# Expert weights and bias rows loaded at other places, the lower split in eight pieces, dest after the lower half, division first at the close

## The reference, cut to what matters

```python
y = (A * p + Bc * vt) / (A * q + Bc)          # per time step; the division of this case
x = layernorm(x + (sigmoid(r) * y) @ Wo.T)    # x1
logits = x @ Wg + bg
score, idx = top_k(logits, 2)                 # softmax over the two
h = tokens @ W1[e] + b1[e]                    # 256 -> 1024
a = gelu(h) if e % 2 == 0 else silu(h)
y_e = a @ W2[e] + b2[e]                       # 1024 -> 256
out = layernorm(x + sum of score * y_e over the two experts)
```

## Time and profile before

| | |
|---|---|
| time, median of 3 runs | 760.79 us (760.13 to 762.02) |
| the profiled execution | 757.0 us |
| its span, first to last instruction | 755.3 us |
| PE busy | 643.4 us, 85% |
| DVE busy | 451.3 us, 60% |
| ACT busy | 393.1 us, 52% |
| POOL busy | 297.3 us, 39% |
| mean granted PE clock | 0.913 of full speed |

### The profile page before, as it was taken

The page is one execution under the profiler, slowest core; times in us unless marked ns, Lnnn a source line. Parts: engine busy times, 40 slices in busy tenths (PEclk is TensorE's granted clock), DMA queues, the critical chain, the costliest instruction groups (busy, mean ns, idle before and its releaser), DMA issues.

```text
span 755.3 us, 14636 instructions
## 1 busy us (share of the span) xinstructions
PE 643.4 (85%) x4472; PEld 600.1 (79%) x4472; DVE 451.3 (60%) x963; ACT 393.1 (52%) x715; POOL 297.3 (39%) x304
## 2 busy tenths in 40 slices
PE   5969799999967659899999999999999999998000
PEld 4858678788755558899999999999999999998000
DVE  4748889999997438455345454454454444442584
ACT  2555566576573132546455464563563645543474
POOL 5100116437446646227253182182531551112364
PEclk9998899999985669899999999999999999999555
DMA  8400222321223492933214123124141121101793
GB/s 254 125 28 1 83 68 74 105 91 65 91 84 120 146 296 56 300 129 113 89 43 155 51 90 114 41 62 144 36 155 51 30 58 44 44 20 33 256 298 125
DMA packets 57111, 78.71 MB, mean 104 GB/s; under 512 B 5190, under 2 KB 46611, under 8 KB 56884
## 3 DMA queue, kind: packets, MB, share of 16 engines
q1 hardware_dynamic: 41540, 51.59, 21.7%
q0 software_dynamic: 6496, 16.99, 6.5%
q10 hardware_dynamic: 8976, 8.72, 4.4%
HBM read 49.14 MB, written 28.92 MB: 103 GB/s over the span
## 4 chain that ended last, share of the span: by engine, by line
PE 73%; DVE 10%; issue 7%; ACT 4%; POOL 2%; DMA 2%; another core or an unknown queue 1%; SPq 0%; DVEq 0%; ACTq 0%; POOLq 0%
PE hT_ps L858 27%; PE y_ps L867 25%; PE vr_ps L711 7%; PE k_ps L711 6%; PE wo_ps L719 2%; PE xT_ps L876 2%; DVE o_all L1201 2%; PE small_ps L733 1%; DVE xl L1279 1%; DMA yy<-expert_out_dram 1%; POOL rstd_c L678 1%; PE xT_ps L779 1%; DVE nd L1208 1%; ACT L1006 1%
## 5 line engine op out<-in xcount | busy, mean ns | idle before, releaser
L858 PE MATMUL hT_ps<-xTh,wx 128*128 128x256 f32 x1120 | 215.3, 290 | 6.0 <-DVE aTl L1179 5.2
L867 PE MATMUL y_ps<-wx,aTh 128*128 128x256 f32 x1088 | 197.5, 283 | 0.9 <-DVE y_sb L1187 0.9
L858 PEld LDWEIGHTS hT_ps<-xTh,wx 128*128 128x128 f32 x1120 | 181.4, 196 | 6.9 <-DVE aTl L1179 5.4
L1179 DVE TENSOR_TENSOR aTl<-hT_ps,aTh 128x512 fp32r<-128x512 f32 x140 | 93.3, 689 | 143.2 <-ACT aTh L1069 139.7
L867 PEld LDWEIGHTS y_ps<-wx,aTh 128*128 128x128 f32 x1088 | 169.7, 192 | 1.2 <-issue 1.1
L659 POOL DMA_INDIRECT expert_out_dram<-y_sb,dest x70 | 68.2, 974 | 251.4 <-DVE y_sb L1187 235.6
L858 PE MATMUL hT_ps<-xTl,wx 128*128 128x256 f32 x560 | 160.9, 287 | 0.0
L867 PE MATMUL y_ps<-wx,aTl 128*128 128x256 f32 x544 | 154.0, 283 | 0.0
L1063 ACT ACT_TABLE_LOAD x33 | 42.3, 1283 | 170.5 <-PE hT_ps L858 161.8
L1063 ACT ACTIVATE hT_ps<-hT_ps,b_c 128x256 f32<-128x256 f32 x280 | 113.5, 468 | 30.4 <-PE hT_ps L858 23.3
L858 PEld LDWEIGHTS hT_ps<-xTl,wx 128*128 128x128 f32 x560 | 110.2, 197 | 0.0
(11 more groups left out here) (194 smaller groups left out, 852.8 us busy)
## 6 DMA issues: line engine op xcount, KB each, us to landing
staging<-in_L_ffn_W SPq DMA_DIRECT2D x16, 1024.0 KB
recs<-records_dram ACTq DMA_DIRECT2D x33, 258.0 KB, 2.8
yy<-expert_out_dram SPq DMA_DIRECT2D x16, 512.0 KB, 5.6
xin<-in_L_attn_x SPq DMA_DIRECT2D x16, 256.0 KB, 4.4
xres<-in_L_attn_x SPq DMA_DIRECT2D x16, 256.0 KB, 3.1
x_dram<-rec SPq DMA_DIRECT2D x16, 256.0 KB, 3.5
xx<-x_dram SPq DMA_DIRECT2D x2, 2048.0 KB
out<-res SPq DMA_DIRECT2D x16, 256.0 KB, 4.0
```

Source lines behind the costliest of these rows:

```text
L858: ins = pe.matmul(hT_ps[b][:, f, :], wx[:, s, part, off:off + P], xpart[t.slot % 2][:, cc, :], start=k == 0, stop=k == len(terms) - 1)
L867: ins = pe.matmul(y_ps[h], apart[t.slot % 2][:, fc, h * P:(h + 1) * P], wx[:, s, part, off:off + C], start=k == 0, stop=k == len(terms) - 1)
L1179: dve.tensor_tensor(aTl[u.slot % 2][:, 2 * b:2 * b + 2, :], hT_ps[b][:], aTh[u.slot % 2][:, 2 * b:2 * b + 2, :].bitcast(F32), ALU.subtract ...
```

## The change

The bias rows b2_b are loaded in SP's step 8, right behind the records of the early blocks, where before they were loaded after the last chunk step. The raw weights of expert 1 are loaded after the padding, the table and all record scatters, and after the records of block 3 have landed (`rec_in[3]`), where before they were loaded right behind the bias rows. The lower part of a split is made in eight operations of 512 columns each. In `halves`, `dest` comes behind xTl, and ACT's load of new records into a buffer waits for `dest_done` in place of `txl_done`. At the close, `divide(7)` moves from the start of DVE's step 8 into step 7, ahead of `choose(5)`; DVE's step 8 does both residuals and the statistics before `choose(6)`; PE's step 8 starts with `project_out(7, 0)`.

```diff
+    LOWER = 8
@@ SP, load_early (step 8)
                     sp.dma_start(recs[n][:], xs[n * BLK:(n + 1) * BLK, :]...).then_inc(rec_in[n], 16)
+                sp.dma_start(b2_b[:], b2.rearrange("(a e) c -> a (e c)", a=1).broadcast_to([P, E * C])).then_inc(bias_in, 16)
@@ SP, after the chunk steps
-            sp.dma_start(b2_b[:], b2.rearrange("(a e) c -> a (e c)", a=1).broadcast_to([P, E * C])).then_inc(bias_in, 16)
-            sp.wait_ge(weights_ready, 1)
-            load_raw(1)
             sp.wait_ge(table, 2)
...
             phase_b_may_start(sp)
-            for e in range(2, E):
+            for e in range(1, E):
                 sp.wait_ge(weights_ready, e)
+                if e == 1:
+                    sp.wait_ge(rec_in[3], 16)
                 load_raw(e)
@@ POOL, split
                 pool.wait_ge(hi_done, e)
-                pool.tensor_tensor(wx[:, e % 2, 1, :], raw[:], wx[:, e % 2, 0, :].bitcast(F32),
-                                   ALU.subtract).then_inc(weights_ready, 1)
+                for n in range(LOWER):
+                    at = bass.ds(n * WE // LOWER, WE // LOWER)
+                    pool.tensor_tensor(wx[:, e % 2, 1, at], raw[:, at], wx[:, e % 2, 0, at].bitcast(F32),
+                                       ALU.subtract).then_inc(weights_ready if n == LOWER - 1 else lower_done, 1)
@@ PE, step 8
                     if i.number == NCH:
+                        project_out(behind, 0)
                         transpose_x1(routed)
-                        project_out(behind, 0)
+                        project_out(behind, 1)
                         score_rows(routed)
-                        project_out(behind, 1)
@@ ACT, loads of records
-            act.wait_ge(txl_done, early_block(0).upto(1))
+            act.wait_ge(dest_done, early_block(0).upto(BH))
...
-                        after(act, txl_done, (u - RING).upto(1))
+                        after(act, dest_done, (u - RING).upto(BH))
@@ DVE, halves
                 dve.tensor_copy(xTh[u.slot % 2][:], xT2_ps[:]).then_inc(txh_done, 1)
+                dve.wait_ge(txh_done, u.upto(1))
+                dve.tensor_tensor(xTl[u.slot % 2][:], xT2_ps[:], xTh[u.slot % 2][:].bitcast(F32),
+                                  ALU.subtract).then_inc(txl_done, 1)
                 after(dve, y_out[u.slot], u.turn(16 * BH))
                 for h in range(BH):
                     dve.scalar_tensor_tensor(... dest ...)
-                dve.wait_ge(txh_done, u.upto(1))
-                dve.tensor_tensor(xTl[u.slot % 2][:], xT2_ps[:], xTh[u.slot % 2][:].bitcast(F32),
-                                  ALU.subtract).then_inc(txl_done, 1)
@@ DVE, steps 7 and 8
                     if i.number == NCH - 1:
-                        stages += [(place, i - 2)]
+                        stages = stages[:-2] + [(divide, i), (choose, i - 2), (place, i - 2)]
                 elif i.number == NCH:
-                    stages = [(divide, i - 1), (residual_0, i - 1), (choose, i - 2), (residual_1, i - 1), (statistics, i - 1),
-                              (place, i - 2)]
+                    stages = [(residual_0, i - 1), (residual_1, i - 1), (statistics, i - 1), (choose, i - 2), (place, i - 2)]
```

More of the change, by code:

```diff
@@ L300, in build @@
         dummy_out = [sem(f"dummy_out{n}") for n in range(2)]
+        lower_done = sem("lower_done")
         known, dest_done, rows_clear = sem("known"), sem("dest_done"), sem("rows_clear")
```

## The result

The changed kernel takes 763.46 us (median of 20 runs, 760.08 to 765.73) against 760.56 us (20 runs, 757.06 to 765.39) for the kernel before in the same rounds: a ratio of 1.0034, with an interval of 1.0018 to 1.0050. That is 2.6 us slower (1.4 to 3.8), where 4.8 had been forecast. The time lies at the lower end of the forecast's own range (763.5 to 767.5); the whole range of 757.0 to 768.0 was wide enough to hold no change as well.

What follows compares the result with a forecast made beforehand. PE was taken as the bound from block 3 on, so product1(4)'s start sets the time: 330.4 against 325.6 us gives +4.8, 757.0 becomes 761.8, and 3.8 to the median gives 765.6. Range 757.0 to 768.0, the forecast's own 763.5 to 767.5.

Steps and rivals of the forecast that it cites:

- Dest and pieces: Second phase: dest behind the lower half and eight pieces start product1(4) 6.2 us earlier; each split takes 1.3 us more.
- T: The time at which the table ends: 290.35 us before, 290.95 with the 0.6 us forecast for the close.
- The close: End of the first phase: spread_of(7) stands behind send_records(5)'s eight scatters on POOL, so everything behind is 0.6 us late.
- The bias rows: SP's 1 MB load behind the early records: lands long before DVE wants it, and nothing waits for it.
- Late weights: Expert 1's late load puts split(1) ahead of block 0's scatters; PE stands 8.5 us before product1(4), at 328.5.
- The clock behind the wait: After its wait ahead of product1(4), PE starts at the lower clock, which costs 1.9 us.
- The sum: Start of product1(4), in effect 330.4 against 325.6 us: +4.8 us in all; chance of the forecast 0.58.
- the unnamed wait goes: Two rivals: ACT's 5.79 us wait at 274.24 disappears, 760.3 us, chance 0.16; it is also longer when timed, 756.5, 0.12.
- the scatters land at once: Rival: block 0's scatters land 3.8 us after the split's end, in place of 8.5; +0.1, 760.9 us, chance 0.08.
- the lower bound: Landing of block 0's scatters with the queues empty: 3.8 us after the split's end, in place of 8.5.
- The close did gain: Rival on the close: the table ends 2.5 us earlier in place of 0.6 later; +1.7, 762.5 us, chance 0.06.

Runs made afterwards that it cites:

- c1: The changed kernel with expert 1's weights loaded early again and the close as before; 753.28 us, 0.9943 of the kernel before.
- b3: The kernel before with dest behind the lower half alone, ACT's loads waiting for dest_done; 754.99 us, 0.9946 of the kernel before.
- b4: The kernel before with the lower split in eight pieces alone; 753.2 us, 0.9916 of the kernel before.
- d1: The kernel before with the lower split in eight pieces and the new close; 752.58 us, 0.9928 of the kernel before.
- b2: The kernel before with the new order of the close alone; 756.26 us, 0.9971 of the kernel before.
- b1: The kernel before with the late load of expert 1's weights alone; 753.77 us, 1.0056 of the kernel before.
- b5: The kernel before with the eight padding writes held until block 0's lower parts are done; 760.95 us in its one run.
- c2: The changed kernel again, unchanged, on another chip; 760.35 us, 1.0026 of the kernel before.
- a3: The changed kernel with the loads of expert 2's weights and x1 held until block 0's scatters have landed; 751.9 us, 1.0024 of the kernel before.
- a1: The changed kernel with expert 1's weights loaded early again, ahead of the padding; 743.85 us, 0.9928 of the kernel before.

## Why the prediction was right, and where it was off

**Dest and pieces.** Right. Either edit alone removes the wait ahead of block 2: product1(4) comes 28.8 us (dest, c1) or 29.9 us (pieces, with dest still ahead) behind T, in place of 34.8 to 35.6. The sum had 6.2 us for both; a stretch of 5.8 us less from T to the end is what c1 and b3 show (459.1 against 464.9), 3.7 to 4.6 what b4 and d1 show. Timed, b3 gained 4.1 and b4 6.4 us. A piece costs 1.26 us, 10.06 for eight against 10.3 in the sum. Each later split is about a microsecond longer, and none of them stands in the chain.

**The close.** Wrong in its term: +0.6 was forecast, -1.4 to -2.2 is what the profiles and b2 give. Two steps failed. The scatters and the handing over were taken 0.6 us too long, so that against the one profile of before the closing is the same. And one execution of before was the only measure: the prediction saw that DVE would be 2.5 us early and lose this in POOL's queue, but not that the old order depended on a wait of POOL for DVE that varies by some 3 us (1.91 us in b1 to 5.22 in b5).

**The bias rows.** Nothing in the chain of the changed kernel waits for them. They weren't tried alone.

**Late weights.** Right in every step, within a microsecond. The records of block 3 landed at T + 5.2 (forecast 5.25), the weights at T + 14.6 (13.85), the split ended at T + 28.5 (27.9), the scatters landed at T + 36.5 (36.4), and product1(4) started at T + 37.55 (37.6). PE's wait was 8.55 us, 8.06 in c2 (8.5). The load took 8.82 us by the chain, the landing 8.0 behind the split's end where 8.5 had been taken; it was 8.0 in c2 too, and 9.3 in b1.

**The clock behind the wait.** 1.9 us had been taken. The first product of block 4 took 2.9 us more than 5.75 in the changed kernel, 2.8 in a3 and 2.0 in c2. In c2 the low stretch ended sooner:

```profile
327.00:331.00 4.00, 4.00 (x20) 0.53 1.10 360
331.00:333.00 2.00, 2.00 (x19) 1.00 1.06 342
```

So the term has a spread of about a microsecond of its own, and the one profile behind the forecast lay at its short end.

**The sum.** From T to the end of the span, the changed kernel takes 470.6 and 469.8 us, the one before 464.9 twice: +5.3, where the forecast's terms behind T make 4.2. The close gives back 1.4 to 2.2. That leaves +3.1 to +3.9, within or just above the measured interval of 1.4 to 3.8. So the mechanism and the sign were right. The time came out lower than forecast because two misses of opposite sign partly cancelled, as far as the profiles can tell: about 1 us more behind T, and 2 to 3 us less at the close. Of the 8.7 us between the two profiles, 3.1 had arisen by the scan of chunk 7 (214.46 against 211.36), before any edit acts.

**The rivals.** In two of them the unnamed wait goes: it stayed, at 6.0 us, and both fall. That the scatters land at once is refuted by 8.0 us from the split's end, and a3 shows what sets it: with SP's next loads held the same two scatters landed after 3.9 us, the lower bound that the prediction had taken from the earlier trace rows. The queues in the changed kernel, 323 to 327 us (packets, MB, share), show only SP's:

```profile
q1 hardware_dynamic: 359, 1.12, 93.5%
```

The Trainium skill's DMA: Bandwidth & Descriptors, section Queues, rings and completion order, has each DMA engine going round between its queues a packet at a time. By that rule a3's edit should have changed little, and it halved the time. POOL's packets came 4 to 5 us behind SP's load in the kernel before and in the changed one. What delays them, the arbitration or something ahead of it, no run shows. The close did gain, but not in the way of its rival: POOL stayed the bound, as the sum had it, and the gain came from the old order's varying wait. Its gain had been put at 2.5 us.

**The best version.** Without the late weights the change gains: a1 took 743.85 us, 0.9928 of before. The pieces alone (0.9916) and pieces with the new close (0.9928) can't be told from it. All three beat the kernel before by 5.4 to 6.4 us, and the changed kernel with it.

## What to carry to other kernels

When a load is made later, follow not only who wants its data but the whole order of the engine that works on it: here the weights were in time to about a microsecond, and the loss came from two scatters that stood behind the split in POOL's queue, whose buffers a third engine wanted. Where two edits each remove the same wait, count it once, and try the smaller alone: eight pieces gave as much as the whole change without its late weights. And a term that is a difference of a few tenths against one profiled execution is not known to its sign: look for what the old order waits for and how far that can vary, before calling it nothing.

## What the hardware showed beyond this

- One kernel differs by more between chips than the change does: the kernel before took 749.5, 757.6, 758.1 and 760.6 us in four sets of 20 to 26 runs. On the chip of 749.5 us all four profiles lack the unnamed wait, which is 3.6 to 6.3 us in the ten others.
- In the profile of before, the matmuls of block 0's later banks have rows that end between 274 and 277 us, and ACT saw them released together at 280.0. It stands in eight of the ten profiles on the slower chips as a wait that has no releaser, and in two as a wait for PE. What holds the releases back is open.
- Executions differ in stages that no edit touches: the scan of chunk 7 starts between 209.0 and 214.5 us, on each of the three chips of the experiments within 1.7 us, and the part behind the last product1 takes 70.9 us in a1 and 72.3 in b4. The timed differences and those of the stretch from T to the end part by up to 3 us either way (b4: 6.4 timed, 3.7 by the stretch; a3: +1.8 timed, +1.0 by the stretch with the close's gain still to come off). So one profile settles a mechanism here, and not a microsecond.
